# Context attentions of layers 1 and 3: scores computed a second time with the keys as rows

## The reference

```python
q = layernorm(x); k = v = ctx_512            # (8, 375, 128)
qh = (q @ Wq + bq).reshape(B, LQ, HEADS, D_K).transpose(0, 2, 1, 3)
kh = (k @ Wk + bk).reshape(B, LKV, HEADS, D_K).transpose(0, 2, 1, 3)
vh = (v @ Wv + bv).reshape(B, LKV, HEADS, D_K).transpose(0, 2, 1, 3)
scores = jnp.einsum('bhqd,bhkd->bhqk', qh, kh) * scale
attn = jax.nn.softmax(scores, axis=-1)
out = jnp.einsum('bhqk,bhkd->bhqd', attn, vh)
x = x + concat(out) @ Wo + bo
```

## Time and profile before

| | |
|---|---|
| runs before, median of 3 | 2270.37 us (2268.21 to 2271.17) |
| the profiled execution | 2266.93 us |
| its span in the profile | 2265.1 us |
| TensorE busy over the span | 2007.5 us (89%) |
| VectorE, ScalarE, GpSimd busy | 1337.6, 906.0, 564.3 us |
| layer 1's context attention | 738.1 to 901.9 us |
| layer 3's context attention | 1987.5 to 2151.9 us |

### The profile page before, as it was taken

The page is one execution under the profiler, slowest core; times in us unless marked ns, Lnnn a source line. Parts: engine busy times, 40 slices in busy tenths (PEclk is TensorE's granted clock), DMA queues, the critical chain, the costliest instruction groups (busy, mean ns, idle before and its releaser), DMA issues.

```text
span 2265.1 us, 57634 instructions
## 1 busy us (share of the span) xinstructions
PE 2007.5 (89%) x22720; PEld 1460.1 (64%) x22720; DVE 1337.6 (59%) x3551; ACT 906.0 (40%) x3432; POOL 564.3 (25%) x1360
## 2 busy tenths in 40 slices
PE   8999999999987898998978888998999999889844
PEld 4899998777566565567866655665644545556623
DVE  6667666665355787545645614876263220678787
ACT  2455554443146565302334523665211111346622
POOL 3566665221011000102345512331000000411111
PEclk9655555999999899899998988999999999889965
DMA  3000001004000000200020000000030000000000
GB/s 139 4 5 5 5 5 57 25 1 186 1 5 2 15 12 27 115 0 24 1 101 37 2 1 8 9 12 1 1 154 0 1 0 0 5 11 12 5 0 16
DMA packets 8025, 57.21 MB, mean 25 GB/s; under 512 B 792, under 2 KB 5248, under 8 KB 5984
## 3 DMA queue, kind: packets, MB, share of 16 engines
q1 hardware_dynamic: 7760, 53.54, 6.2%
HBM read 52.62 MB, written 0.92 MB: 24 GB/s over the span
## 4 chain that ended last, share of the span: by engine, by line
PE 68%; DVE 14%; ACT 7%; issue 6%; POOL 4%; DMA 1%; POOLq 0%; DVEq 0%; SPq 0%; ACTq 0%
PE banks L269 44%; PE banks L274 7%; PE banks L1390 6%; PE banks L963 3%; ACT memory L1011 2%; PE banks L989 2%; DVE memory L1492 2%; PE banks L1543 1%; ACT memory L1417 1%; POOL memory L1449 1%; ACT memory L1424 1%; DVE memory L1273 1%; DVE memory L1498 1%; DVE memory L1501 1%; DVE memory L850 1%
## 5 line engine op out<-in xcount | busy, mean ns | idle before, releaser
L269 PE MATMUL banks<-memory 128*112 128x256 f32 (+8 forms) x4192 | 1127.2, 424 | 98.8 <-DVE memory L3540 21.8
L269 PEld LDWEIGHTS banks<-memory 128*128 128x128 f32 (+3 forms) x4192 | 699.1, 194 | 433.6 <-issue 279.5
L274 PE MATMUL banks<-memory 112*125 112x112 f32 (+3 forms) x2000 | 299.8, 282 | 80.2 <-DVE memory L850 24.9
L274 PEld LDWEIGHTS banks<-memory 112*125 112x125 f32 (+3 forms) x2000 | 233.7, 169 | 194.7 <-issue 109.0
L1390 PE MATMUL banks<-memory 128*128 128x8 bf16 (+2 forms) x10752 | 306.7, 174 | 14.2 <-DVE memory L1475 1.4
L1390 PEld LDWEIGHTS banks<-memory 128*128 128x128 bf16 x10752 | 295.6, 104 | 25.9 <-POOL memory L1449 23.8
L1011 ACT ACTIVATE memory<-banks,memory 112x375 f32<-112x375 f32 x384 | 215.4, 579 | 25.4 <-DVE memory L1049 25.3
L1049 DVE TENSOR_REDUCE memory<-banks 112x2 f32<-112x750 f32 x192 | 171.0, 933 | 39.1 <-PE banks L963 38.9
L1492 DVE TENSOR_REDUCE memory<-banks 128x48 f32<-128x192 f32 x448 | 121.7, 290 | 61.6 <-PE banks L1390 47.4
L1057 DVE COPY memory<-banks 125x448 f32<-125x448 f32 x192 | 117.0, 619 | 8.1 <-PE banks L274 3.6
L1571 ACT ACTIVATE memory<-memory 112x112 f32<-112x112 f32 x192 | 71.7, 375 | 90.5 <-DVE memory L1592 90.5
(11 more groups left out here) (240 smaller groups left out, 2467.2 us busy)
## 6 DMA issues: line engine op xcount, KB each, us to landing
memory<-in_l2x SPq DMA_DIRECT2D x1, 7680.0 KB, 21.7
memory<-in_l2f SPq DMA_DIRECT2D x1, 7168.0 KB, 20.0
memory<-in_l1f SPq DMA_DIRECT2D x1, 4617.0 KB, 15.8
memory<-in_ctxT SPq DMA_DIRECT2D x24, 187.5 KB
memory<-in_l2f SPq DMA_DIRECT2D x1, 4096.0 KB, 12.7
memory<-in_l3f SPq DMA_DIRECT2D x1, 3073.0 KB, 22.6
memory<-in_l2a SPq DMA_DIRECT2D x1, 3072.0 KB, 19.2
memory<-in_l0f SPq DMA_DIRECT2D x1, 2304.0 KB, 9.1
```

The lines of the kernel that those rows point to most:

```text
L269: ins = self.nc.tensor.matmul(out, weights[i], acts[i], start=i == 0, stop=i == n - 1)
L274: return self.nc.tensor.transpose(out, in_, self.ident[0:n, 0:n])
```

## The change

Heads are worked in pairs, 8 to a batch and 64 to a stage. Pair n (`pair`) has a half h of the partitions (two strips), parity m, tile t and two of the six banks 0 to 5. In the words of the code, per pair:

- `cross` of pair n: TensorE computes the scores of pair n+2 as before (two products, 375 columns; `score`) and between them those of pair n with the keys stationary (six products, 125 columns by 112 queries; `turned_score`). VectorE takes the maxima of pair n+2, negated, into `peaks`; ScalarE takes one exponential over both heads (125 by 672) with no bias and no sum; GpSimd adds the three key chunks in two additions (`esum`).
- `peak` of pair n: TensorE waits for the maxima, transposes `peaks` (112 by 128), VectorE adds the result to the queries. The keys now exist once per parity too, with the other head's channels 0 but one of them 1 (`mask`, `k_shift`), so that the turned scores come out less their maximum.
- `weighted`: 12 products as `values4`, straight from the exponentials, and four products of ones by `esum`, which give the sums of weights in bank 6.
- `norm`: a reciprocal of 128x224 from the bank and a product. `share`, `inverse`, all copies of transposed weights and 12 transposes a group are gone.
- `kk` takes the place of `k`: two ScalarE operations instead of one. `ring` is bank 7 alone.

```diff
-    plan = ((("inverse", 0, -1), ("xT", 0, 1)),
-            (("q", 0, 1), ("k", 0, 1)),
-            (("y", 0, -1), ("k", 1, 1), ("stats", 0, 2)),
-            (("vv", 0, 1), ("v", 2, 1), ("xn", 0, 2)))
+    plan = ((("xT", 0, 1), ("stats", 0, 2)), (), (("q", 0, 1),), (("kk", 0, 1), ("xn", 0, 2), ("y", 0, -1)), (), (),
+            (("vv", 0, 1),), (("kk", 1, 1), ("v", 2, 1)))
...
+        self.pack, self.ring = pack, (7,)
...
+    def order(self):
...
+        for n in range(self.pairs):
+            b, i = divmod(n, 8)
+            if n + 1 < self.pairs:
+                yield "peak", (n + 1) // 8, n + 1
+            yield "cross", b, n
+            if n >= 4 and n % 4 < 2:
+                yield "weighted", (n - 4) // 8, (n - 4) // 4 * 2 + n % 4
+            if b and i == 1:
+                yield "norm", b - 1, 0
+            for kind, at, ahead in self.plan[i]:
+                if 0 <= b + ahead < B:
+                    yield kind, b + ahead, at
...
+        if step == "kk":
+            self.wait_keys(b)
+            src, w = self.key_source(), self.w_k
+            bank = k.next_bank(("k", b, i), s.k_ready(KD * b + i + 1))
...
+        elif step == "peak":
+            b, t, m, h, x = self.pair(i)
+            PE.wait_ge(*s.nmax_ready(i + 1))
+            k.tp(k.banks[:, x, 384:384 + S], self.peaks[:, 2 * m + h, :]).then_inc(*s.peak_full.up())
+        elif step == "cross":
+            n, more = i, i + 2 < self.pairs
+            if more:
+                self.pe_score_waits(n + 2)
+            PE.wait_ge(*s.peak_ready(n + 1))
+            for r in range(2):
+                if more:
+                    ins = self.score(n + 2, r)
+                    if r:
+                        ins.then_inc(*s.sc_full.up())
+                self.turned_score(n, r, 0)
+                self.turned_score(n, r, 1)
+            self.turned_score(n, 2, 0)
+            self.turned_score(n, 2, 1).then_inc(*s.turned_full.up())
...
+    def act_more(self, step, b, i, u):
...
+            for m in range(2):
+                ins = A.activation(u["kT"][:, i, m, :], bk, ACT.Identity, bias=self.k_shift[:, m, i:i + 1],
+                                   scale=self.mask[:, m:m + 1])
+            ins.then_inc(*s.k_ready.up())
...
+            V.wait_ge(*s.peak_full(i + 1))
+            V.tensor_tensor(q, k.banks[rows, x, 384:384 + S], q, ALU.add).then_inc(*s.peak_ready.up())
+        elif step == "norm":
+            V.wait_ge(*s.val_full(4 * (b + 1)))
+            V.reciprocal(self.R, k.banks[:, 6, KD * S:2 * KD * S]).then_inc(*s.vstep.up())
+            V.wait_ge(*s.vstep.now())
+            V.tensor_tensor(self.oT.rearrange("p t s -> p (t s)"), k.bank(6, P, KD * S), self.R,
+                            ALU.mult).then_inc(*s.oT_ready.up())
```

More of the change, by code:

```diff
@@ L1970, in __init__ @@
         super().__init__(k)
-        self.pack = pack
+        self.pack, self.ring = pack, (7,)
         w = self.w = k.packs[pack]
@@ L1979, in __init__, with pair @@
         self.take_parity(take)
+        self.mask, self.one, self.k_shift = take(2), take(2), take(2, KD)
+        self.ones = take(2, 32)
+    def pair(self, n):
+        b, i = divmod(n, 8)
+        t, j = divmod(i, 4)
+        return b, t, j % 2, j // 2, 2 * (n % 3)
+    def order(self):
+        for kind, i in self.prologue:
+            yield kind, 0, i
+        yield "score", 0, 0
+        yield "score", 0, 1
+        for kind, i, b in self.second:
+            yield kind, b, i
+        yield "peak", 0, 0
+        for n in range(self.pairs):
+            b, i = divmod(n, 8)
+            if n + 1 < self.pairs:
[8 more added lines that the diff above has]
+                    yield kind, b + ahead, at
+        yield "weighted", B - 1, 4 * B - 2
+        yield "weighted", B - 1, 4 * B - 1
+        yield "norm", B - 1, 0
+        for kind, i in self.epilogue:
+            yield kind, B - 1, i
@@ new lines, in score, with turned_score @@
+    def score(self, n, r):
+        b, t, m, h, x = self.pair(n)
+        u, rows = self.bufs[b % 2], slice(64 * h + 32 * r, 64 * h + 32 * r + 32)
+        return self.nc.tensor.matmul(self.k.bank(x + r, S, CK), u["q"][rows, m, t, :], u["kT"][rows, t, m, :],
+                                     start=True, stop=True)
+    def turned_score(self, n, c, r):
+        b, t, m, h, x = self.pair(n)
+        u, rows = self.bufs[b % 2], slice(64 * h + 32 * r, 64 * h + 32 * r + 32)
+        return self.nc.tensor.matmul(self.k.banks[0:CR, x + r, c * S:(c + 1) * S],
+                                     u["kT"][rows, t, m, c * CR:(c + 1) * CR], u["q"][rows, m, t, :],
+                                     start=True, stop=True)
@@ new lines, in dve_peaks, with dve_more @@
+    def dve_peaks(self, n):
+        s, V = self.s, self.nc.vector
+        b, t, m, h, x = self.pair(n)
+        if n == 0:
+            V.wait_ge(*s.zeroed(3))
+        at = 64 * h + 16 * (1 - m)
+        V.wait_ge(*s.sc_full(n + 1))
+        V.tensor_reduce(self.peaks[:, 2 * m + h, at:at + 33:32], self.k.banks[0:S, x:x + 2, 0:CK], AX, ALU.max,
+                        negate=True).then_inc(*s.nmax_ready.up())
+    def dve_more(self, step, b, i, u):
+        k, s, V = self.k, self.s, self.nc.vector
+        if step == "score":
+            self.dve_peaks(i)
+        elif step == "cross":
+            if i + 2 < self.pairs:
+                self.dve_peaks(i + 2)
+        elif step == "peak":
+            b, t, m, h, x = self.pair(i)
+            rows = slice(64 * h, 64 * h + 64)
+            q = self.bufs[b % 2]["q"][rows, m, t, :]
+            V.wait_ge(*s.peak_full(i + 1))
[6 more added lines that the diff above has]
+                            ALU.mult).then_inc(*s.oT_ready.up())
+        elif step == "kk":
+            pass
+        elif step == "weighted":
+            pass
+        else:
+            super().dve_more(step, b, i, u)
@@ new lines, in pool_more @@
+    def pool_more(self, step, b, i, u):
+        s, G = self.s, self.nc.gpsimd
+        if step == "parity":
+            for u in self.bufs:
+                G.memset(u["v"], 0.0).then_inc(*s.zeroed.up())
+            G.memset(self.ones, 0.0).then_inc(*s.gstep.up())
+            G.memset(self.peaks, 0.0).then_inc(*s.gstep.up())
+            G.wait_ge(*s.gstep.now())
+            for m in range(2):
+                ins = G.memset(self.ones[:, m, 16 * m:16 * m + 16], 1.0)
+            ins.then_inc(*s.zeroed.up())
+        elif step == "cross":
+            b, t, m, h, x = self.pair(i)
+            gi = 4 * b + 2 * t + m
+            eT, esum = self.eT[gi % 3][0:CR, 2 * h:2 * h + 2, :], self.esum[gi % 3][0:CR, 2 * h:2 * h + 2, :]
+            G.wait_ge(*s.exp_done(i + 1))
+            if gi >= 3:
+                G.wait_ge(*s.val_full(gi - 2))
+            G.tensor_tensor(esum, eT[:, :, 0:S], eT[:, :, S:2 * S], ALU.add).then_inc(*s.gstep.up())
+            G.wait_ge(*s.gstep.now())
+            G.tensor_tensor(esum, esum, eT[:, :, 2 * S:3 * S], ALU.add).then_inc(*s.esum_ready.up())
```

92 lines of the change are left out of this document (87 added, 5 removed).

## The result

The changed kernel takes **2355.09 us** (2353.91 to 2357.41), the kernel before 2269.73 beside it: a ratio of 1.0372 [1.0351, 1.0393], slower by 85 us where the forecast said 64. The profiled execution took 2357.4 us, against 2266.9 before. Every ratio in this document leaves out one disturbed execution of 6224 us, of e8_plan_late_ring.

A forecast was written before the change was run, and what follows sets the result against it. TensorE's own work was taken to bound the kernel before, at 18.5 us a batch. With the change's round trips and waits a batch takes 22.9: stages +33 and +31, +64 on 2266.9, median 2334 us, range 2312 to 2350 (0.58).

The forecast's parts named there:

- Each slot has a round trip through VectorE: Per pair, `cross` start to next: scores 0.93, reduction 0.93, answer 0.05, transpose 0.28; 2.2 us, at least 17.7 a batch.
- Slot 2, `norm`: Third slot of a batch: `norm`, ending slot 1, delays VectorE's next maxima by 1.0, so the slot takes 3.2 us.
- Slots 3 and 7, bank 7: `y` and `v` wait for ScalarE's two reads of `kk` in bank 7; the slots take 4.2 and 3.8 us.
- TensorE's own sum: TensorE's work in a batch, added up without waits: 17.6 us, 0.9 less than the 18.5 now.
- first `cross` into the stage: Prologue: first scores at 8.6 us as now, then VectorE's operations bring the first `cross` to about 16.6 us.
- first batch: First eight pairs of a stage, without `norm` and `y`: 19.4 us.
- batches 1 to 6: Steady middle of a stage: 22.9 us a batch against 18.5 now, 137 us together.
- last batch and tail: End of a stage: 15.0 us to its last `cross`, then 9.1 for exponential, sums, two `weighted`, `norm` and `y`.
- Rival 1: In `cross`, strips with products of different length don't run apart: 1.4 us instead of 0.83, 2392 us in all; chance 0.16.
- Rival 2: TensorE's clock falls where slots 3, 4 and 7 idle: 8 us a stage, 2350 us in all; chance 0.13.
- Rival 3: Bank 7 is no wait: slots 3 and 7 lose 1.5 us each, 2290 us in all; chance 0.08.
- Rival 4: Faster: maxima, bank 7 and `norm` hidden behind TensorE's work, 14 us less, 2256 us in all; chance 0.05.

The follow-up runs named there:

- e8_plan_late_ring: Changed kernel with side work replanned across slots, `peak` of pair n+1 behind `cross` n, and banks 4 and 5 added to the prologue's ring: 1.0130 of the kernel before.
- e9_half_reduce: Changed kernel with maxima taken over only the first 187 of 375 keys of each score: 1.0270 of the kernel before.
- e5_less_pe: Changed kernel without eight of the twelve value products of each `weighted` step: 1.0371 of the kernel before.
- e1_copy: Changed kernel with `norm` copying the sums of weights instead of taking their reciprocal: 1.0281 of the kernel before.
- e4_y_slot5: Changed kernel with `y` moved from slot 3, behind `kk`, to slot 5: 1.0302 of the kernel before.
- e2_kk3: Changed kernel with ScalarE reading each `kk` bank a third time, into a spare buffer: 1.0562 of the kernel before.
- e6_prologue_ring: Changed kernel with banks 4 and 5 beside bank 7 for projections up to the first `cross`: 1.0344 of the kernel before.
- e11_plan_ring: Changed kernel with side work replanned across slots and banks 4 and 5 beside 7 in the prologue, `peak` still before `cross`: 1.0122 of the kernel before.
- e3_late_peak: Changed kernel with `peak` of pair n+1 behind `cross` n and VectorE's reduction behind the addition: 1.0427 of the kernel before.
- e10_y5_late: Changed kernel with `peak` of pair n+1 behind `cross` n and `y` in slot 5 instead of 3: 1.0301 of the kernel before.

## Why the prediction was right, and where its sizes were off

**What held.** The direction, the mechanism and the range. *"Each slot has a round trip through VectorE"*: 2.2 us forecast and 2.21 measured in every slot without other load; e9_half_reduce shortens it by shortening the reduction, e5_less_pe shows that less work for TensorE does not. *Slot 2, `norm`*: 3.2 and 3.17; e1_copy takes it away with the reciprocal. *Slots 3 and 7, bank 7*: 4.2 and 3.8 against 4.26 and 3.84; e4_y_slot5 takes slot 3's away, e2_kk3 makes both longer. Behind these waits `y` takes 0.93 and `v` 0.50 from start to start, against the 0.96 and 0.53 that were worked out. The addition (0.27 against 0.268), the exponential (0.73, 0.732), the reciprocal (1.56, 1.550) and GpSimd's additions (0.66; 0.658 and 0.608) measured as taken from the rows, or close to it. TensorE's own sum was 0.5 too small (18.1, not 17.6), which the waits hide.

**What was mis-sized: the ends of the stage.** Layer 1's stage by the terms of the forecast, from the end of the stage before at 737.09 to its own end at 944.33:

| term | forecast | measured |
|---|---|---|
| first `cross` into the stage | 16.6 | 21.1 |
| (of these, up to the first scores) | 8.6 | 9.9 |
| first batch | 19.4 | 22.5 |
| batches 1 to 6 | 137 | 136.5 |
| last batch and tail | 24.1 | 27.2 |
| stage | 197 | 207.2 |

- *"The first scores come at 8.6 us as now"* (+1.3; +0.4 in layer 3). The change puts small VectorE operations, the masks and the shifts of the keys, at the head of the stage, beside GpSimd's memset (737.20 to 739.90). One of 128x2 elements is in the trace with 2.84 us; the kernel before ran one of the same size at 743.79, with no memset beside it, in 0.17. `stats` starts only behind them, at 740.89. The scaling that the earlier trace rows shows with 2.75 us beside the memset now takes 0.41 behind it, so most of the delay comes back, but not all.
- *"two reductions, `stats`, `vv`, `v`, `xn` and an addition bring the first `cross` to about 16.6"* (+3.1 more, 11.1 from the first scores instead of 8.0). I added VectorE's operations, but the path runs through bank 7 here as well: `kk` at 749.77, `vv` at 752.79 behind ScalarE, `v` at 755.78 behind VectorE, each at the lower clock. I had counted bank 7's waits in the batches and forgotten them in the prologue. e6_prologue_ring, which takes these waits away and leaves the lower clock, has 8.1 in both layers, the forecast's sum.
- *"the first batch has no `norm` and no `y`: 19.4"* (+3.1). Its first three slots are 3.02, 3.05 and 3.71, since the clock comes back only at 767.95. In layer 1 of e11_plan_ring, without the prologue's waits, it is back at 753.43, and the first four slots are 2.18, 2.21, 2.21 and 2.21. In layer 3 of the same run it is back only 27 us into the stage, and the slots are 3.02, 3.05 and 3.71. So the clock is what makes these slots long, and the waits alone do not decide when it comes back.
- *The last batch and the tail* (+3.1): with nothing for a next batch TensorE is idle more, and the clock is at the lower level from 924.96 for 3.4 us and again from 935.2 to the end.
- *The rest of the span "keeps its time"*: it lost 4 us, mostly in the stages behind. I put that down to the same clock: between layer 1's stage and the end of layer 2's self attention it is at the lower level for 45.5 us, before the change for 37.5. No run here separates that.

That makes 10.7 us in layer 1's stage less 0.5 gained in the batches, some 12 in layer 3 and 4 elsewhere: 26 on the span. The median stood 3.4 us above the profiled execution before and stands 2.3 below it now, which takes 6 off and leaves the 21 of the miss, to 1 us.

**The rivals.** Rival 1 is refuted by the rows of `cross`. Rival 2, the clock, was right in kind and wrong in place: in the steady batches it stays at 1.00 although TensorE is idle 1.4 us at bank 7, and it falls at the ends; over the stage it comes to 0.90, just at the sign that was named for it (under 0.9). e2_kk3 and e3_late_peak show how near the batches are to it as well. Rival 3 is refuted by the 1.40. Rival 4 fails by the 22.8 us of a batch: neither the maxima nor bank 7 nor `norm` are hidden, and TensorE's work is not smaller either (18.13 us busy against 17.85).

**GpSimd beside VectorE.** Two rows of the timelines of VectorE and GpSimd in a steady batch, and before them the same operation in the prologue, where GpSimd was idle:

```profile
742.40 0.41 DVE L855 TENSOR_SCALAR memory<-memory 112x256 f32<-112x256 f32 x1 [0.67 <-POOL memory L871]
...
790.50 0.85 DVE L855 TENSOR_SCALAR memory<-memory 112x256 f32<-112x256 f32 x1
...
790.54 0.66 POOL L2196 TENSOR_TENSOR memory<-memory 125x224 f32<-125x224 f32 x1 [1.86 <-ACT memory L2118]
```

`xn` takes twice its time beside GpSimd's addition, in all six batches of layer 1 (0.852 on the mean) and in the six of layer 3. By the Trainium skill, SBUF — State Buffer, section on the two separate sides, that is the port pair, which whichever operation starts first holds for its whole length while the other waits. The trace agrees that the two don't run freely side by side, but not with the order: `xn` is on record 0.04 us before the addition, and yet it is `xn` that takes 0.44 longer, while the addition keeps its 0.66. It fell into VectorE's slack. The other place where I had let it cost up to 5 us, layer 1's second `y` operation (L841), kept its 0.425 in all six batches; no GpSimd instruction ran beside it there, so the rule for two inputs is not tested by it.

**What stays open.** Of the 28 us that e11_plan_ring is behind the kernel before, 0.8 a batch is 13; the rest lies in prologues, tails and their clock, and I did not try to take it away. No run computed the scores one pair further ahead, which should hide the round trip, down to TensorE's own work (2.0 us in a slot with `weighted`, by e9_half_reduce): it needs two more banks, and three pairs of scores, the values and the ring hold all eight.

## What to carry to other kernels

A change can lower the work of two engines (ScalarE from 12.5 to 8.3 us a batch, VectorE from 16.3 to 15.8), add next to nothing to TensorE's and still lose, if it ties two engines into a round trip per small tile: write down first the loop (scores, maxima, transposed maxima, next scores) and its length, and only then the sums. Whatever stands on the middle engine of such a loop is paid as soon as it is longer than the slack there (`norm` at 1.95 us cost 1.0, at 0.8 nothing), and a wait at the one bank that the loop's projections share holds up the whole loop; so when a chain becomes serial, the order of the side work has to be planned anew (here it gave back half of the loss). And work out the prologue and the tail by the same waits as the steady state, with TensorE's clock at the level that the trace shows for stretches with as little work.

## What the runs showed of the hardware that I had not expected

- **A wait can cost again when the clock falls behind it.** With a wait of 1.40 us and TensorE busy 2.00 of 3.40 us around it, the clock stayed at 1.00 in every steady batch of the changed kernel. With a wait of 1.96 (busy 1.44 of 3.40) it fell to 0.50 for 3.4 us in eight places of one stage, and each fall cost about 1.4 us more. No one number of these tells a fall: with the late `peak` the same waits were in every batch and falls behind only some of them, one of them after a stretch (799.20 to 802.60 of e10_y5_late) with TensorE busy 2.00 of 3.40.
- **Row strips are independent.** A product of 375 columns on one strip and one of 112 on another start within 0.01 us of each other, and the short ones go on starting every 0.1 us while a long one's first pass, 0.40 us from start to start, is under way; two scores and six turned scores, in two passes each, are through in 0.84 us.
- **The reciprocal is the expensive one.** Over 128x224 from a bank it takes 1.55 us, a copy 0.38 and a product 0.39 over the same elements (e1_copy).
